# Attention denominators and router logits: the small matrix made stationary in four column strips of TensorE, with a copy and one matmul per group to turn the result back

## The reference, cut to what matters

```
h   = layernorm(x) * (1 + ca) + sa                    # modulation rows from c @ wmod
q   = h @ Wq ;  feat = elu(q) + 1                     # (n, l, 8, 16)
Ksum = feat.sum(axis=1)
Z   = 1 / (einsum('nlhd,nhd->nlh', feat, Ksum) + 1e-6)        # the denominators
msg = einsum('nlhd,nhdv,nlh->nlhv', feat, KV, Z) ... @ Wm
x   = h + layernorm(msg) ... + layernorm(relu(msg @ W1) @ W2) ... ; x = x_in + ga * x
h   = layernorm(x) * (1 + cb) + sb
logits = h @ Wg                                       # 8 experts: the router logits
probs = softmax(logits); each expert takes its top 512 tokens; every token goes to one expert
x   = x + gb * gate * (gelu(h @ W1[e]) @ W2[e])
```

## Time and profile before

| | us |
|---|---|
| median of 3 runs | 232.7 |
| profiled execution, its time | 233.51 |
| profiled execution, its span (first to last instruction) | 231.7 |
| TensorE busy | 175.6 |
| VectorE busy | 171.6 |
| ScalarE busy | 132.4 |
| GpSimd busy | 152.0 |

### The profile page before, as it was taken

One profiled execution on the slowest core, in us unless ns is written; L12 is line 12 of the kernel. 1 busy time (PEld: TensorE's weight loads), 2 busy tenths in 40 slices (PEclk: granted clock), 3 DMA queues, 4 the chain that ended last, 5 costly groups with the idle time before them and its releaser, 6 DMA issues.

```text
span 231.7 us, 4342 instructions
## 1 busy us (share of the span) xinstructions
PE 175.6 (76%) x1161; PEld 138.6 (60%) x1161; DVE 171.6 (74%) x661; ACT 132.4 (57%) x425; POOL 152.0 (66%) x236
## 2 busy tenths in 40 slices
PE   0779898999999998965664869877589989985000
PEld 0536676888778887854333446555379879974000
DVE  1889988699998798998988989998018997554000
ACT  2149985367647897854987853332547667851000
POOL 8698837357266868454799950057777787777771
PEclk9999999999999999975577577999999999999555
DMA  5995000000100000000176222013343352111110
GB/s 166 263 280 200 3 0 1 0 3 0 46 3 0 4 0 0 1 3 0 39 203 204 83 82 74 0 33 104 91 112 91 98 127 81 46 61 45 57 45 23
DMA packets 16967, 15.49 MB, mean 67 GB/s; under 512 B 1904, under 2 KB 14320, under 8 KB 16944
## 3 DMA queue, kind: packets, MB, share of 16 engines
q1 hardware_dynamic: 14288, 9.70, 14.0%
q0 software_dynamic: 2240, 5.51, 8.1%
q10 hardware_dynamic: 416, 0.01, 0.1%
HBM read 8.92 MB, written 6.29 MB: 66 GB/s over the span
## 4 chain that ended last, share of the span: by engine, by line
PE 34%; DVE 33%; POOL 15%; issue 7%; ACT 6%; DMA 2%; POOLq 1%; DVEq 0%; ACTq 0%
POOL out_dram L422 7%; PE pH L974 6%; DVE scr L1315 6%; PE pQ L983 6%; DVE x_sb L1190 4%; POOL yr L287 4%; DVE bn L1022 3%; PE pQ L881 3%; DVE rows L1030 2%; POOL rs L287 2%; DMA x_sb<-in_L_attn_x_dram 2%; PE pH L871 2%; DVE mv L1025 2%; PE pH L804 1%; DVE featT L1044 1%
## 5 line engine op out<-in xcount | busy, mean ns | idle before, releaser
L419 POOL DMA_INDIRECT rows<-table_dram,gidx x28 | 30.0, 1072 | 24.2 <-DVE gidx L1407 16.0
L422 POOL DMA_INDIRECT out_dram<-rows,gidx x28 | 27.3, 976 | 8.5 <-issue 6.7
L974 PE MATMUL pH<-x_sb,hid 128*128 (+1 forms) x140 | 22.5, 283 | 1.1 <-ACT hid L637 0.9
L983 PE MATMUL pQ<-ew,u 128*128 (+1 forms) x140 | 22.2, 281 | 1.2 <-ACT u L651 0.8
L373 POOL TENSOR_TENSOR scr<-feat,z 128x512 f32<-128x512 f32 x8 | 8.8, 1098 | 18.0 <-DVE z L1167 18.0
L983 PEld LDWEIGHTS pQ<-ew,u 128*128 128x128 f32 x140 | 18.4, 191 | 3.0 <-issue 1.9
L651 ACT ACTIVATE u<-pH 128x256 f32<-128x256 f32 x35 | 13.4, 384 | 11.5 <-PE pH L974 11.4
L1456 DVE SCALAR_TENSOR_TENSOR t<-pQ,wslot,scr 128x128 f32<-128x128 f32 x35 | 12.2, 347 | 10.5 <-PE pQ L983 10.0
L974 PEld LDWEIGHTS pH<-x_sb,hid 128*128 128x128 f32 x140 | 18.4, 191 | 2.3 <-issue 2.1
L524 ACT ACTIVATE sqj<-pQ 128x128 bf16<-128x128 f32 x60 | 15.8, 281 | 6.6 <-PE pQ L815 3.0
L287 POOL TENSOR_TENSOR yr<-yv,neghalf 128x4 f32<-128x4 f32 x16 | 17.6, 1099 | 1.3
(11 more groups left out here) (331 smaller groups left out, 530.8 us busy)
## 6 DMA issues: line engine op xcount, KB each, us to landing
table_dram<-x_sb SPq DMA_DIRECT2D x9, 256.0 KB, 2.8
x_sb<-in_L_attn_x_dram SPq DMA_DIRECT2D x8, 256.0 KB, 5.6
table_dram<-rows SPq DMA_DIRECT2D x7, 256.0 KB, 2.4
ew<-in_L_ffn_W_dram SPq DMA_DIRECT2D x2, 512.0 KB, 9.1
w1d<-in_L_ffn_W_dram SPq DMA_DIRECT2D x1, 1024.0 KB, 10.4
rows<-table_dram,gidx POOLq DMA_INDIRECT x28, 2.8
out_dram<-rows,gidx POOLq DMA_INDIRECT x28, 2.2
wmod_sb<-in_L_wmod_dram SPq DMA_DIRECT2D x1, 384.0 KB, 4.7
```

The source lines that it names most:

```text
L419: gp.indirect_dma_start(row[:, t, :], None, table[:, :], bass.IndirectOffsetOnAxis(gidx[:, t:t + 1], 0)).then_inc(gathered[t], 16)
L422: gp.indirect_dma_start(out.rearrange("b l d -> (b l) d"), bass.IndirectOffsetOnAxis(gidx[:, t:t + 1], 0), row[:, t, D:2 * D], None).then_ ...
L974: mm = te.matmul(pH[i % 2][:, f * P:(f + 1) * P], wcur[:, i % RW, f * P:(f + 1) * P], xt[:, bass.ds(i - e, 1), :], start=True, stop=True)
L983: mm = te.matmul(pQ[i % 2][:, 0:D], eh[:, i % 2, f * P:(f + 1) * P], ew[:, bass.ds(e, 1), f * D:(f + 1) * D], start=(f == 0), stop=(f == 1))
```

## The change

`ksel` and `wgc` become 32 columns wide (HQ = 32, eight used, the rest set to zero by two memsets on GpSimd at the start). For all eight groups of the denominators, and for groups 0 to 5 of the logits (TILED = 6), the small matrix is now stationary and the activations are moving: tile t of the group goes to partitions 32t to 32t+31 of the result (`den_raw`, `lg_raw`), which is a column strip of TensorE. The result has heads (or experts) on partitions and tokens on columns. It is copied to SBUF (`denS` by VectorE in `v_den`, with the 1e-6 added there; `lgS` by ScalarE in `a_lg`), and one matmul per group, with the copy stationary and the columns `heads` of the identity moving, turns it back to tokens on partitions (`p_den_tok`, `p_lg_tok`). `v_z` is then the reciprocal alone.

The orders change with it. On TensorE `p_y1` is cut in two, and `p_den_tok(s)` stands between `p_y1(s-2)` and the MLP matmuls `p_m1(s-2)`; `p_lg_tok(s-5)` stands after `p_y2(s-3)` and `p_lg(s-5)`, ahead of `p_tx3(s-4)`. On VectorE `v_den(0)` stands ahead of `v_feat(7)`, `v_den(s)` at the head of steps 1 to 7, and the reciprocals of groups 1 to 3 come later in their steps: that of group 1 after `v_ksum(1)`, that of group 2 after `v_acc(1)`, that of group 3 after `v_kvt(1)` and `v_acc(3)`; `v_u1(1)` follows that. On ScalarE `a_lg(s-5)` stands after `a_relu` and `a_soft`, ahead of `a_xn3` and of the squares of y2.

```diff
...
 E, F = 8, 256
+HQ = 32
 CAP = B * L // E
...
 DG = G - 1
+TILED = G - 2
 SOFT = ((0, slice(0, TB)), (1, slice(0, TB - GT)), (1, slice(TB - GT, TB)))
...
         cbR = sb("cbR", [P, B, D]); dgb = sb("dgb", [P, D])
-        wgs = sb("wgs", [P, B, E]); wgc = sb("wgc", [P, B, E]); cR = sb("cR", [P, B, E])
+        wgs = sb("wgs", [P, B, E]); wgc = sb("wgc", [P, B, HQ]); cR = sb("cR", [P, B, E])
         bsum = sb("bsum", [P, D]); rowm = sb("rowm", [P, 4])
...
         xn = rows2[:, 0, :, :].rearrange("p (g t) d -> p g t d", t=GT); h2T = sb("h2T", [P, 2, W]); hT = scr[:, 20:28, :].rearrange("p (a t) d -> p a (t d)", t=GT); ex = sb("ex", [P, 2, W])
-        ksp = sb("ksp", [P, G]); ksum = sb("ksum", [P, B]); ksel = sb("ksel", [P, B, H]); kdiag = sb("kdiag", [P, B, P])
+        ksp = sb("ksp", [P, G]); ksum = sb("ksum", [P, B]); ksel = sb("ksel", [P, B, HQ]); kdiag = sb("kdiag", [P, B, P])
         gts = sb("gts", [P, B, P]); kvt = sb("kvt", [P, B, P]); mall = sb("mall", [P, B, D + F])
+        denS = sb("denS", [P, P]); lgS = sb("lgS", [P, P])
         z = sb("z", [P, 2, GT * H]); qp = scr[:, 12:20, :].rearrange("p (a t) d -> p a (t d)", t=GT); qT = sb("qT", [P, 2, W])
...
             ks_done gts_done kv_ready kvt_done mall_ready mall_done
-            den_ready z_done qp_done tq qT_done y1_ready m1_ready relu0 y2_ready sq1 sq2 u1_done u2_done yr1_done yr2_done x1_done
+            den_raw den_sb den_ready lg_raw lg_sb z_done qp_done tq qT_done y1_ready m1_ready relu0 y2_ready sq1 sq2 u1_done u2_done yr1_done yr2_done x1_done
             wgs_done cm_ready wgc_done stats3 rs3 nm_done xn3 tx3 h2_done txd h2_last lg_ready
...
             return (pL, pF)[g // GB][:, g % GB * GT * E:(g % GB + 1) * GT * E]
+
+        den_raw, den_tok = pG[:, 0:P], pG[:, P:P + GT * H]
+        lg_raw = pL[:, 2 * P:3 * P]
+        heads = ident[:, :].rearrange("p (t c) -> p t c", c=HQ)[:, :, 0:H]

...

+            gp.memset(ksel[:, :, :], 0.0)
+            gp.memset(wgc[:, :, :], 0.0)
             gp.memset(onesb[:, :], 1.0)
...

+            def a_lg(g):
+                act.wait_ge(S["lg_raw"], g + 1)
+                if g >= 1:
+                    act.wait_ge(S["lg_ready"], g)
+                act.copy(lgS[:, :], lg_raw[:, :]).then_inc(S["lg_sb"], 1)
+
             def a_xn3(g, ts=range(GT)):
...
                     a_square(s - 3, 1, "y2_ready", "sq2")
+                if 0 <= s - 5 < TILED:
+                    a_lg(s - 5)
                 if 0 <= s - 6 < ACT_ROWS:
...
                 for t in range(GT):
-                    mm = te.matmul(pG[:, t * H:(t + 1) * H], featT[:, (g * GT + t) * P:(g * GT + t + 1) * P],
-                                   ksel[:, b, :], start=True, stop=True)
-                mm.then_inc(S["den_ready"], 1)
+                    mm = te.matmul(den_raw[t * HQ:(t + 1) * HQ, :], ksel[:, b, :], featT[:, (g * GT + t) * P:(g * GT + t + 1) * P],
+                                   start=True, stop=True)
+                mm.then_inc(S["den_raw"], 1)
+
+            def p_den_tok(g):
+                te.wait_ge(S["den_sb"], g + 1)
+                te.matmul(den_tok, denS[:, :], heads, start=True, stop=True).then_inc(S["den_ready"], 1)

...
                     p_gt(s - 3)
+                if s == G:
+                    p_den_tok(0)
                 if s == 5:
...
             p_tq(0)
+            p_den_tok(1)
             p_gt(G - 1)
...
                 mm.then_inc(S["y1_ready"], 1)
+
+            def p_m1(g):
+                b = g // GB
                 if g >= 1:
...
                     te.wait_ge(S["qT_done"], G)
+                if g < TILED:
+                    if g == GB:
+                        te.wait_ge(S["lmax"], 1)
+                    for t in range(GT):
+                        mm = te.matmul(lg_raw[t * HQ:(t + 1) * HQ, :], wgc[:, g // GB, :], h2T[:, g % 2, t * P:(t + 1) * P],
+                                       start=True, stop=True)
+                    mm.then_inc(S["lg_raw"], 1)
+                    return
                 for t in range(GT):
-                    mm = te.matmul(lg_out(g)[:, t * E:(t + 1) * E], h2T[:, g % 2, t * P:(t + 1) * P], wgc[:, g // GB, :],
+                    mm = te.matmul(lg_out(g)[:, t * E:(t + 1) * E], h2T[:, g % 2, t * P:(t + 1) * P], wgc[:, g // GB, 0:E],
                                    start=True, stop=True)
                 mm.then_inc(S["lg_ready"], 1)
+
+            def p_lg_tok(g):
+                te.wait_ge(S["lg_sb"], g + 1)
+                te.matmul(lg_out(g), lgS[:, :], heads, start=True, stop=True).then_inc(S["lg_ready"], 1)

...
                     p_y1(s - 2)
+                    if s < G:
+                        p_den_tok(s)
+                    p_m1(s - 2)
                 if 0 <= s - 5 < G and s <= G:
...
                     p_lg(s - 5)
+                if 0 <= s - 5 < TILED:
+                    p_lg_tok(s - 5)
                 if 0 <= s - 4 < G:
...
                 link(dve.reduce_sum(ksum[:, b:b + 1], ksp[:, b * GB:(b + 1) * GB], AX.X))
-                dve.tensor_scalar(ksel[:, b, :], same16[:, 0:P:HD], ksum[:, b:b + 1], None, ALU.mult)
+                dve.tensor_scalar(ksel[:, b, 0:H], same16[:, 0:P:HD], ksum[:, b:b + 1], None, ALU.mult)
                 dve.tensor_scalar(kdiag[:, b, :], ident[:, :], ksum[:, b:b + 1], None, ALU.mult).then_inc(S["ks_done"], 1)
...
                 dve.wait_ge(S["wgs_done"], 1)
-                dve.scalar_tensor_tensor(wgc[:, :, :].rearrange("p b e -> p (b e)"), pH1[:, 400:400 + B * E], -1.0 / D,
-                                         wgs[:, :, :].rearrange("p b e -> p (b e)"), ALU.mult, ALU.add)
+                dve.scalar_tensor_tensor(wgc[:, :, 0:E], pH1[:, 400:400 + B * E].rearrange("p (b e) -> p b e", e=E), -1.0 / D,
+                                         wgs[:, :, :], ALU.mult, ALU.add)
                 dve.tensor_copy(cR[:, :, :].rearrange("p b e -> p (b e)"), pH1[:, 416:416 + B * E]).then_inc(S["wgc_done"], 1)
...

+            def v_den(g):
+                dve.wait_ge(S["den_raw"], g + 1)
+                if g >= 1:
+                    dve.wait_ge(S["den_ready"], g)
+                dve.tensor_scalar(denS[:, :], den_raw, ATTN_EPS, None, ALU.add).then_inc(S["den_sb"], 1)
+
             for s in range(G + 1):
+                if s == G:
+                    v_den(0)
                 if 0 <= s - 1 < G:
...
                     dve.wait_ge(S["qp_done"], g - 1)
-                link(dve.tensor_scalar(z[:, g % 2, :], pG[:, 0:GT * H], ATTN_EPS, None, ALU.add))
-                dve.reciprocal(z[:, g % 2, :], z[:, g % 2, :]).then_inc(S["z_done"], 1)
+                dve.reciprocal(z[:, g % 2, :], den_tok).then_inc(S["z_done"], 1)

...
             for s in range(G + 4):
-                if s < 4:
+                if 1 <= s < G:
+                    v_den(s)
+                if s == 1:
+                    v_ksum(1)
+                if s < 2:
                     v_z(s)
                 if s == 1:
-                    v_ksum(1)
                     prep_scales()
...
                     v_acc(1)
+                    v_z(s)
                 if s == 3:
                     v_kvt(1)
+                    v_acc(3)
+                    v_z(s)
                     v_u1(1)
-                    v_acc(3)
                 if 0 <= s - 6 < ACT_ROWS:
...
                 if 0 <= s - 4 < G:
```

## The result

The changed kernel takes 236.6 us (median of four runs, 236.1 to 237.2) against 232.8 us. The ratio is 1.0152, 95% interval 1.0129 to 1.0175; timed a second time, beside other kernels, it was 1.0179 (1.0130 to 1.0229). That is 3.5 to 4.2 us, where I had forecast 1.2.

A forecast was written before the change was run, and what follows sets the result against it. The prediction took TensorE as the bound to about 56 us, then the VectorE-GpSimd loop to 95. Its terms, +0.5 +0.6 -0.65 +0.75 = +1.2 us, gave 233.9 us from 232.7, range 231.0 to 237.0.

The forecast's parts named there:

- 56 to 67 us: Middle stage: TensorE waits 1.7 us for VectorE's copy of group 4, making u2(1) and x1(1) late; +0.6 us.
- the loop's gain: VectorE-GpSimd loop (x1, z, qprime, rsqrts) loses the 1e-6 addition, 0.22 us, for groups 5, 6 and 7: -0.65 us.
- rival B: Strips run one after another or drain; a unit of 1.1 to 1.4 us lengthens TensorE's steps; about 236.5 us, chance 0.27.
- What bounds the stage: Middle stage: TensorE on the chain to about 56 us, then the VectorE-GpSimd loop to 95, though TensorE is busy throughout.
- the direction: Whole kernel: forecast slower by 1.2 us; chances slower 0.48, same 0.37, faster 0.15.
- TensorE's price of a unit: One group's small product: strips 0.55 plus turning matmul 0.20, so 0.75 against 0.79 us before; range 0.42 to 1.43.
- Up to 56 us: Start of middle stage: `v_den(0)` ahead of `v_feat(7)`, later qprime(1), TensorE's wait for `v_den(3)`; together +0.5 us.
- rival D: Half clock, starting at about 100 us, starts elsewhere; up to 3 us hang on it; widens the range, no separate chance.
- 67 to 90 us: Middle-stage steps where the VectorE-GpSimd loop sets the pace: shorter without the addition, -0.65 us.
- 90 to 102 us: Stage end: ScalarE's `a_lg(4)` waits for strips, delaying y2(6)'s squares, GpSimd's rsqrt and x1(6)'s second half; +0.75 us.
- Rival C: No change: new waits fall into unseen slack and the shorter loop pays for the rest; 232.9 us, chance 0.2.

The follow-up runs named there:

- e10: Kernel before, with one logit matmul in place of four for groups 0 to 5, so less TensorE work and wrong logits; ratio 0.9986.
- e7: Logits of groups 0 to 5 as in the change, denominators as in the kernel before; 234.5 us, ratio 1.0066.
- e1: The change, with `v_den(4)` moved from the head of step 4 to between `v_u2(0)` and `v_acc(4)`; 236.0 us, ratio 1.0108.
- e3: The change, with only the logits of groups 0 to 3 through the strips (TILED = 4); 234.9 us, ratio 1.0062.
- e5: The change with `v_den(4)` ahead of `v_acc(4)` and only the logits of groups 0 to 3 through the strips; 233.9 us, ratio 1.0035.
- e2: The change, with two filler matmuls of 512 columns ahead of the turning matmul of group 4; 236.7 us, ratio 1.0129.

## Why the prediction was wrong, step by step

The step that failed is the one from 56 to 67 us: it has the wait, but not the half clock behind it. It is not the whole miss, for every other delay was priced too small as well (1.15 for 0.5, 0.97 for 0.6 and 1.15 for 0.75 us), and the loop's gain too large (0.50 for 0.65). The wide range, 231.0 to 237.0, holds the measured 236.6 us only through rival B, whose mechanism did not come: that is luck.

- **What bounds the stage** was right, and e10 shows it for steps 5 to 10. So was the direction.
- **TensorE's price of a unit**: 0.35 us for strips instead of 0.55, some 0.1 to 0.2 us of gaps ahead of the strips and behind the turning matmul that I had left out of the likeliest value, 0.14 to 0.24 for the turning matmul; 0.7 in all where I had 0.75. The Trainium skill ("TensorE: Matmul & The Clock Gate", Part 3) says that column strips run side by side; the trace agrees, with four matmuls that start within 0.02 us. The Trainium skill ("TensorEngine Tiling (Array Packing)", Key Properties) says that a change of mode drains the engine; the trace agrees in kind, with 0.10 us ahead of the strips and 0.09 behind them, about half of the 0.17 us tail that I had taken for a drain. In this stage it didn't matter. Rival B's price (1.1 to 1.4) was refuted although its time, 236.5, is the one that came.
- **Up to 56 us** was mis-sized. u2(0) is 0.95 us later on the ruler, beside the 0.2 of `v_den(0)` ahead of it, which makes 1.15 where I had 0.5 for both. Three waits of TensorE cost 0.31 (qprime(1)), 0.34 (qprime(2)) and 0.33 us (`denS` of group 3): the first I had priced at 0.1, the second not seen, and only the last priced in full. The whole shift of the last `v_feat` was 0.65 us; 0.45 of it arose before 37 us, where the two kernels differ by two memsets. The same start came between 40.96 and 41.80 us in the profiles of the variants that have the strips from group 0 on, and at 41.40 us in e10, whose front is that of the kernel before (40.87). So this is scatter of that stage, unexplained.
- **56 to 67 us** is the step that failed. The wait was there, 1.85 us for 1.7, and by itself it cost 0.97 us where I had 0.6. What I did not have is that TensorE's clock is granted at half behind it in some executions, which makes two matmuls 1.7 us longer right on the chain. My rival D let the half clock start in another place, but priced it by the logits and transposes at the end of the stage, and tied it to no wait. A wait that I had worked out to within 0.15 us stood before me, and I asked only who is late after it, not what the idle engine does next.
- **67 to 90 us** was right: -0.51 (x1(1) to x1(4): 21.38 against 21.89) for -0.65.
- **90 to 102 us** had the right cause and the wrong follower: 1.15 us instead of 0.75. I followed the late squares to GpSimd's rsqrt, which had slack. VectorE's own u2(6) waits for the same squares (1.08 us in e7), and both halves of x1(6) are queued behind it.
- **Rival C**, that the new waits fall into slack, is refuted by e1 and e3: without the one wait and without the other the stretch is shorter by 0.97 and 1.16 us.

The sum of the middle stage, by the ruler: +0.88 (start, as in e1 at x1(1)), +0.97 (the wait), -0.50 (the loop), +1.15 (ScalarE) = 2.50, the second profile of the change; with the half clock 2.50 + 1.70 = 4.20, the first profile (65.95 - 61.76 = 4.19). The terms are differences of the same ruler, so that they add up is no evidence by itself. The evidence is in the kernels that lack one or two of the delays: e7, which has only ScalarE's, is 1.22 late, and e5, without the wait and without ScalarE's, came at 62.07 where 62.0 to 62.4 was expected. With the 0.2 of `v_den(0)` the sum is 2.7 or 4.4 us, on either side of the 3.5 to 4.2 measured. So even without the half clock the terms come to 2.7 where I had 1.2. The eight runs of the change fall into 235.9 to 236.1 and 237.1 to 238.3 us, four each, which would fit a half clock that comes in about half of them, and the two profiles of the change agree (237.16 us with it, 236.08 without). But it is not shown: the kernel before scatters too, from 232.0 to 234.0 us, and e2, with the same stretch and full clock, took 236.96.

What stays open: how often the half clock comes, and how much of the measured loss is due to it. Behind the middle stage, from the start of the rank search to the end of the span, the kernels need between 119.2 and 121.4 us (before 120.2, the change 119.2, e1 121.4), with the same program. TensorE's clock changes there in different places from profile to profile; I did not take this apart, and it is as large as the differences that a time of one kernel can show. An idle of 1.85 us was followed by half clock in two profiles of four; what decides it was not tried.

## What to carry to other kernels

An engine that is busy all the time can still be off the path, and then making its work cheaper can be worth nothing, as here: follow the chain first, or take work away from it and see whether the stage moves, as e10 did. What a rewrite costs lies in the new hand-overs; place each copy on the other engine's queue by when its reader wants it, ahead of work that nobody waits for. And when an inserted wait leaves TensorE idle for a microsecond or two, count the matmuls behind it at half clock as a case with a chance of its own.

## What the runs showed of the hardware

- Four strips of 32 columns, eight pairs of weight load and 128-column float32 matmul in all, take 0.35 us from their start to that of what follows; the same eight pairs with a full 128-column stationary matrix take 0.89 us. Their weight loads take 0.11 us each, where full ones take 0.19 (L842, 194 ns in the mean on the page of the changed kernel):

```profile
L738 PEld LDWEIGHTS pG<-featT,ksel x64: 106/108/111, 39.8 to 81.6; 128*32 128x32 f32 x64
L738 PE MATMUL pG<-featT,ksel x64: 272/284/298, 39.8 to 81.7; 128*32 128x128 f32 x64
```

- The eight start in two waves of four, 0.13 us apart, and not in the five slots of 0.11 us that I had thought of.
- The strips start 0.10 us later than a matmul of the usual form behind the same instruction, and the matmul behind them starts 0.20 us after their last instead of 0.11.
- After TensorE had idled 1.85 us its granted clock was 0.50 for 3.3 us in two of four profiles, and full in the two others and in both with work in the gap.
